# The local mask of the last attention stage: added by VectorE in PSUM instead of multiplied in by TensorE

## The reference, cut to what matters

```
DIM, DEPTH, HEADS, DIM_HEAD, WINDOW, QK_SCALE = 128, 6, 16, 64, 32, 8.0
def local_attention(q, k, v):            # q, k, v: b, h, n, d; n = 256 in windows of 32
    bq = q.reshape(b, h, nw, w, d)
    bk2, bv2 = look(bk), look(bv)        # each window sees itself and the one before: 64 keys
    mask = (it < jb) | (it > jb + w) | (jb == -1)
    sim = jnp.einsum('bhwie,bhwje->bhwij', bq, bk2) * QK_SCALE
    sim = jnp.where(mask, -jnp.finfo(sim.dtype).max, sim)
    attn = jax.nn.softmax(sim, -1)
    return jnp.einsum('bhwij,bhwje->bhwie', attn, bv2).reshape(b, h, n, d)
def attn_layer(x, ...):
    q, k, v = split(x @ Wqkv[i])         # 128 -> 3 x 1024
    q, k = l2norm(q) * qs, l2norm(k) * ksc   # then the rotary turn with its scales
    return local_attention(q, k, v) @ Wo[i]
def ffn_layer(x, ...):                   # layer norm, then a * gelu(gate)
    a, gate = split(xn @ W1[i] + b1[i])
    return a * jax.nn.gelu(gate, approximate=False) @ W2[i] + b2[i]
for i in range(DEPTH):
    x = attn_layer(shift_tokens(x), ...) + x
    x = ffn_layer(shift_tokens(x), ...) + x
```

## Time and profile before

| | |
|---|---|
| median of 3 runs | 4949.91 us (4947.79 to 4951.49) |
| the profiled execution | 4954.48 us, of which the span from the first to the last instruction is 4953.2 us |
| mean granted TensorE clock in it | 0.977 of full speed |
| last stage (`L3f`) | from about 1650 us to the end |
| busy: PE, PEld, DVE, ACT, POOL | 4669.7, 3168.2, 3438.3, 3509.7, 3707.7 us |

### The profile page before, as it was taken

The page is one execution under the profiler, slowest core; times in us unless marked ns, Lnnn a source line. Parts: engine busy times, 40 slices in busy tenths (PEclk is TensorE's granted clock), DMA queues, the critical chain, the costliest instruction groups (busy, mean ns, idle before and its releaser), DMA issues.

```text
span 4953.2 us, 115870 instructions
## 1 busy us (share of the span) xinstructions
PE 4669.7 (94%) x45088; PEld 3168.2 (64%) x45088; DVE 3438.3 (69%) x4939; ACT 3509.7 (71%) x6742; POOL 3707.7 (75%) x2336
## 2 busy tenths in 40 slices
PE   6999789996888699999999999999999999999997
PEld 4665558884444366666666666666666666666665
DVE  4553446665999677777777777777777777777774
ACT  2443655554777478778888888888877888887885
POOL 1111224445999789999999999999999999999993
PEclk9999889997999899999999999999999999999999
DMA  0000000002343222232222222232223222222222
GB/s 23 2 1 1 7 14 1 1 1 112 139 170 137 58 62 53 65 78 61 63 65 67 69 65 62 54 82 66 54 65 78 61 64 65 67 69 65 61 54 50
DMA packets 163477, 288.98 MB, mean 58 GB/s; under 512 B 44143, under 2 KB 60278, under 8 KB 158838
## 3 DMA queue, kind: packets, MB, share of 16 engines
q1 hardware_dynamic: 161926, 281.18, 21.6%
q10 hardware_dynamic: 1008, 0.39, 0.0%
HBM read 90.09 MB, written 2.62 MB: 19 GB/s over the span
## 4 chain that ended last, share of the span: by engine, by line
PE 64%; ACT 1%; POOL 1%; issue 1%; DVE 1%; DMA 0%; ACTq 0%; DVEq 0%
PE ps L2461 21%; PE ps L2519 8%; PE ps L2493 8%; PE ps L2474 7%; PE ps L2532 7%; PE ps L2506 4%; PE ps L2558 3%; PE ps L2574 3%; PE ps L2565 2%; PE ps L2488 2%; PE ps L2545 1%; PE ps L2539 1%; POOL L3f_t L3049 0%; POOL L3f_raw L3066 0%; DMA L3f_qks<-in_L_ffn_k_scale 0%
## 5 line engine op out<-in xcount | busy, mean ns | idle before, releaser
L3049 POOL TENSOR_TENSOR L3f_t<-L3f_raw,L3f_rot 128x512 f32<-128x512 f32 x768 | 1100.7, 1456 | 291.3 <-DVE L3f_raw L2876 288.8
L2461 PE MATMUL ps<-L3f_wqkv,all_z 128*128 128x512 f32 x2304 | 1171.9, 608 | 31.1 <-DVE L3f_raw L2876 22.4
L3066 POOL TENSOR_TENSOR L3f_raw<-L3f_raw,L3f_t 128x1024 f32<-128x1024 f32 x384 | 954.8, 2487 | 3.8
L3058 POOL TENSOR_TENSOR L3f_raw<-L3f_raw,L3f_rot 128x1024 f32<-128x1024 f32 x384 | 910.1, 2370 | 3.8
L2876 DVE TENSOR_TENSOR L3f_raw<-ps,L3f_ri 128x512 f32<-128x512 f32 x768 | 507.2, 682 | 273.6 <-ACT L3f_ri L2683 250.2
L2859 DVE TENSOR_REDUCE L3f_ss<-L3f_sqr 128x8 f32<-128x512 f32 x768 | 510.3, 679 | 218.3 <-ACT L3f_sqr L2673 217.1
L2704 ACT ACTIVATE L3f_qz<-ps 64x512 f32<-64x512 f32 x768 | 450.8, 587 | 179.0 <-PE ps L2474 174.4
L2474 PEld LDWEIGHTS ps<-all_ident,L3f_raw 128*128 128x128 f32 x3072 | 371.1, 141 | 293.7 <-issue 263.8
L2461 PEld LDWEIGHTS ps<-L3f_wqkv,all_z 128*128 128x128 f32 x2304 | 386.7, 191 | 263.4 <-issue 165.2
L2673 ACT ACTIVATE L3f_sqr<-ps 128x512 f32<-128x512 f32 x768 | 452.5, 596 | 67.7 <-PE ps L2461 61.3
L2725 ACT ACTIVATE L3f_pT<-ps 64x512 f32<-64x512 f32 x768 | 454.0, 591 | 55.4 <-PE ps L2506 46.4
(11 more groups left out here) (342 smaller groups left out, 8564.9 us busy)
## 6 DMA issues: line engine op xcount, KB each, us to landing
L3f_vw<-L3f_v SPq DMA_DIRECT2D x1344, 128.0 KB, 2.4
L3a_Bs<-L3a_rows SPq DMA_DIRECT2D x16, 2048.0 KB, 7.1
L3a_Cs<-L3a_rows SPq DMA_DIRECT2D x16, 2048.0 KB, 11.6
L3f_vw<-L3f_v SPq DMA_DIRECT2D x192, 64.0 KB, 2.1
L3f_wqkv<-in_L_ffn_Wqkv SPq DMA_DIRECT2D x24, 256.0 KB, 2.8
L3f_wqkv<-in_L_ffn_Wqkv SPq DMA_DIRECT2D x6, 512.0 KB, 3.6
L3f_wo<-in_L_ffn_Wo SPq DMA_DIRECT2D x48, 64.0 KB, 2.3
out<-all_x SPq DMA_DIRECT2D x8, 256.0 KB, 3.1
```

The lines of the kernel that those rows point to most:

```text
L2461: p.matmul(PS[:, j % 3, :], Z[:, u % NSEQ, t * P:t * P + P], w, start=True, stop=True).then_inc(proj.sem)
L3049: op = g.tensor_tensor(t[:, :, to], r[:, :, fr], w[:, 1, to].unsqueeze(1).broadcast_to((P, H, WIN)), ALU.mult)
L3058: g.tensor_tensor(r, r, w[:, 0, :].unsqueeze(1).broadcast_to((P, H, HD)), ALU.mult).then_inc(cosined.sem)
L3066: g.tensor_tensor(r, r, t, ALU.add).then_inc(rotated.sem)
```

## The change

The two bf16 mask products ahead of the scores are gone; the 64 score products write the banks afresh. A new VectorE step `hidden(u, t)` waits for the scores and adds `lmaskb` to banks 6 and 7 in place, broadcast over the heads; it raises a new semaphore `s_mask`, for which `top` now waits. The four lists are printed in a new order. The rest of the diff consists of such moves; TensorE's list is shown as it now stands (the step names alone, (0) for the even unit 2i, (+1) for 2i+1, and so on).

```
@@ scores, on TensorE
-                for b in range(2):
-                    p.matmul(PS[:, 6 + b, :], self.identb[:, :], lmaskb[:, t, b, :].unsqueeze(1).broadcast_to((P, PAIRS, KEYS)),
-                             start=True, stop=False, skip_group_check=True)
                 for a in range(PAIRS):
                     for w in range(NW):
                         r = slice(w % 2 * HD, w % 2 * HD + HD)
                         mm = p.matmul(PS[r, 6 + w // 2, a * KEYS:(a + 1) * KEYS], qz[:, t, a, w, :, :].rearrange("p h q -> p (h q)"),
-                                      kT[:, a, t * P + w * WIN:t * P + w * WIN + KEYS], start=False, stop=True, skip_group_check=True)
+                                      kT[:, a, t * P + w * WIN:t * P + w * WIN + KEYS], start=True, stop=True)
                 mm.then_inc(scored.sem)
@@ on VectorE
+            def hidden(u, t):
+                if not 0 <= u < N:
+                    return
+                v.wait_ge(*scored.at(u, t))
+                x = PS[:, 6:8, :].rearrange("p b (a k) -> p b a k", k=KEYS)
+                v.tensor_tensor(x, x, lmaskb[:, t, :, :].unsqueeze(2).broadcast_to((P, 2, PAIRS, KEYS)), ALU.add).then_inc(s_mask.sem)
+
             def top(u, t):
                 if not 0 <= u < N:
                     return
-                v.wait_ge(*scored.at(u, t))
+                v.wait_ge(*s_mask.at(u, t))
```

More of the change, by code:

```diff
@@ L2591, in turn_back @@
                     mm.then_inc(z_turned.sem)
-            project_out(2 * i)
+            project(2 * i + 2, "v1b")
+            ffn_up(2 * i - 1, 0)
+            ffn_up(2 * i - 1, 1)
+            ffn_up(2 * i - 1, 2)
+            centre(2 * i)
+            project(2 * i + 3, "q0a")
+            project(2 * i + 3, "q0b")
+            turn_qk(2 * i + 2, 0, 0)
+            project(2 * i + 3, "k0a")
+            variance(2 * i)
             turn_qk(2 * i + 2, 0, 1)
[L2595 to L2598, removed]
             turn_back(2 * i - 1, range(FINAL - 1))
@@ L2650, in pe @@
             ffn_gate(2 * i + 1, 1)
-            project(2 * i + 4, "v1b")
             ffn_gate(2 * i + 1, 2)
[L2653 to L2659, removed]
+            project_out(2 * i + 2)
         def act(i):
@@ L2777, in gelu @@
                     a.preload_act_table_set(EXP_LN)
[L2779 removed]
+            value(2 * i + 2, "v1a")
+            gelu(2 * i - 1, 0)
+            gelu(2 * i - 1, 1)
+            gelu(2 * i - 1, 2)
+            centred(2 * i)
+            value(2 * i + 2, "v1b")
+            squared(2 * i + 3, "q0a")
+            squared(2 * i + 3, "q0b")
             turned(2 * i + 2, 0, 0)
@@ L2956, in dve @@
                 rotation(2 * i // NSEQ + 1)
-            sums(2 * i + 3, "k0a")
+            total(2 * i + 1, 1)
             share(2 * i + 1, 0)
+            share(2 * i + 1, 1)
+            norm(2 * i + 2, "k1a")
+            norm(2 * i + 2, "k1b")
+            scale(2 * i + 1, 0)
+            residual(2 * i)
+            gated(2 * i - 1, 0)
+            gated(2 * i - 1, 1)
+            gated(2 * i - 1, 2)
+            sums(2 * i + 3, "q0a")
+            sums(2 * i + 3, "q0b")
+            bounded(2 * i + 3, "q0")
+            scale(2 * i + 1, 1)
             norm(2 * i + 3, "q0a")
-            residual(2 * i)
             norm(2 * i + 3, "q0b")
[L2962 to L2967, removed]
+            normal(2 * i)
             land(2 * i - 1, range(FINAL - 1))
@@ L2970, in dve @@
             land(2 * i - 1, range(FINAL - 1, FINAL))
-            normal(2 * i)
-            share(2 * i + 1, 1)
-            scale(2 * i + 1, 1)
+            sums(2 * i + 3, "k0a")
+            sums(2 * i + 3, "k0b")
+            bounded(2 * i + 3, "k0")
+            norm(2 * i + 3, "k0a")
+            norm(2 * i + 3, "k0b")
+            hidden(2 * i + 2, 0)
+            top(2 * i + 2, 0)
             sums(2 * i + 3, "q1a")
             sums(2 * i + 3, "q1b")
-            top(2 * i + 2, 0)
             bounded(2 * i + 3, "q1")
+            norm(2 * i + 3, "q1a")
+            norm(2 * i + 3, "q1b")
             below(2 * i + 2, 0)
-            norm(2 * i + 3, "q1a")
             sums(2 * i + 3, "k1a")
-            norm(2 * i + 3, "q1b")
             sums(2 * i + 3, "k1b")
@@ L2992, in dve @@
             norm(2 * i + 4, "q0a")
+            sums(2 * i + 4, "k0a")
+            share(2 * i + 2, 0)
+            residual(2 * i + 1)
+            norm(2 * i + 4, "q0b")
+            sums(2 * i + 4, "k0b")
             total(2 * i + 2, 1)
-            share(2 * i + 2, 0)
-            norm(2 * i + 4, "q0b")
-            residual(2 * i + 1)
             scale(2 * i + 2, 0)
-            sums(2 * i + 4, "k0a")
-            sums(2 * i + 4, "k0b")
             bounded(2 * i + 4, "k0")
```

130 lines of the change are left out of this document (60 added, 70 removed).

## The result

The changed kernel takes 4898.6 us (median of 4 runs, 4895.76 to 4900.73) beside 4950.7 us for the kernel before: a ratio of 0.9887 with a 95% interval of [0.9863, 0.9911]. That is 52 us less by the medians and 56 by the ratio. The forecast was 4879 us. The time lies in the range, 20 us above the forecast and just above what rival A allowed (4862 to 4895), at the lower edge of rival B's price.

What follows compares the result with a forecast made beforehand. TensorE's packed order in the last stage was taken to bound the kernel. From 4954.5 us profiled, less 80 for the mask products, plus 9 for waits, gives 4883, about 4879 us as median; range 4855 to 4940 us.

Steps and rivals of the forecast that it cites:

- rival A: Last stage: TensorE stays packed, with small waits only; 4862 to 4895 us, chance 0.68.
- rival B: New lists too tight: late norms, turns and `spread` take 0.85 us an iteration; 4910 us (4895 to 4940), chance 0.16.
- What bounds the kernel: Last stage: TensorE's order is packed, iteration 67.08 us; the stage costs the sum of its streams.
- rival D: No change: GpSimd's chain sets the period, iteration stays about 67 us; 4950 us, chance 0.06.
- The cost of a mask pair, 0.43 us: In `scores`, two 512-column bf16 products cost 0.43 us a call, 187 packed calls: 80 us.
- the low end of the range: No waits, long `scale` gone, `values` and `scores` side by side sharing a change of tile: 4855 us.
- `hidden` at 1.22 us, off TensorE's path: VectorE's mask add takes 1.22 us a call, 5.04 us an iteration with starts, beside TensorE's work.
- the charge for the orders: New lists: a few places even within 0.3 us cost 0.2 us an iteration, 9 us.
- its sign: Profile after: TensorE waits naming ScalarE's turned or spread outputs would point to rival B.
- The place that it watched most closely: Behind `project_out(2i+1)`, before `scores(2i+3, 1)`: VectorE needs 12.7 us, TensorE 12.8, even within 0.3 us.
- What the profile after would show: No L2488, TensorE 800 of 800 us, iteration 65.4 to 65.7 us, VectorE near 54.5, `hidden` 1.22.
- Fill and drain: Outside the packed stretch: new worth as much as old within 3 us; long `scale` 7 us both ways.

Runs made afterwards that it cites:

- f3: f1's lists, but masking by the two bf16 products on TensorE and no VectorE add: 4928.3 us, ratio 0.9955.
- f1: Changed kernel with all four lists laid out anew by its own profile's durations, every step kept: 4823.4 us, ratio 0.9745.
- e2: Changed kernel with its new lists, without the VectorE add, so no mask at all: 4896.0 us, ratio 0.9885.
- e3: Kernel before with its old lists, the VectorE add straight ahead of each row maximum replacing the mask products: 4909.9 us, ratio 0.9912.
- e1: Kernel before with its old lists, the two mask products taken out and no mask in their place: 4879.9 us, ratio 0.9853.
- x2: Changed kernel with the add done twice in each call: 4935.8 us, ratio 0.9972.
- e4: Changed kernel's new lists, masking by the two bf16 products on TensorE as before, no add: 4991.2 us, ratio 1.0076.
- x1: Changed kernel without the first of four ScalarE copies of `spread` in the even unit's first half: 4868.0 us, ratio 0.9837.
- f2: Changed kernel with all four lists laid out anew, a second layout with somewhat more distance between steps: 4876.5 us, ratio 0.9853.

## Why the prediction was right, and where its sizes were wrong

- **What bounds the kernel** was right. With the products gone and no waits the iteration falls by all that they cost (f3 to f1), with GpSimd at 761 of 800 us; rival D is out.
- **The cost of a mask pair, 0.43 us,** was right for the calls that stand alone. Where `values` comes directly before, it is 0.69. The prediction had seen that these two could share a change of tile, and put it only into the low end of the range. The removal was worth 1.99 us an iteration, not 1.72. The Trainium skill's 131 ns for a product ("TensorE: Matmul & The Clock Gate", Back-to-back issue gap) in a real stream would have made it an estimated 1.05; the 0.43 us for two products here, 0.215 each, do not bear it out.
- **`hidden` at 1.22 us, off TensorE's path,** was right (1.224 us; e2 against the changed kernel: no difference). That holds for the new lists; in the old ones the add costs 30 us (e3 against e1). x2 shows that of 5.04 us more an iteration 4.1 would be hidden too.
- **The step that failed is the charge for the orders: "I charge 0.2 us an iteration for them, 9 us."** It measured 0.86 us an iteration and 38 us (e4 against before). That this is half of 1.72, what rival B took, is chance; but the mechanism is B's, turns that wait for ScalarE behind `spread` and `turned`, and the prediction had named those outputs as its sign. So what came true is in the main the rival that it gave 0.16, and the range held because it took B in; A, given 0.68, was missed by 4 us. The place that it watched most closely, VectorE behind `project_out(2i+1)`, did not wait: from `residual` to the end of `below` VectorE took 12.2 us (3169.74 to 3181.94), not 12.7, and `scores(2i+3, 1)` started 1.2 us later, 0.70 of which was the wait for ScalarE. Without that wait (x1) it does not wait either. It had laid VectorE's and GpSimd's lists beside TensorE's in numbers, and not ScalarE's.
- That the forecast is only 20 us off is partly luck, since the two errors partly cancel: forecast 67.08 - 1.72 + 0.2 = 65.56, measured 67.07 - 1.99 + 0.86 = 65.94. The profiled execution was to be 71 us shorter and was 53.8. The 17 us are 45 x 0.38 = 17, 3 for the iterations with `rotation` and 2.6 for counting 46.7 packed iterations where 45 are, less the 5.6 that fill and drain gave. The rest of the 20 is that the median lies 2 us below the profiled execution, not 4.6.
- **What the profile after would show:** `hidden` at 1.22, no L2488, 0.09 us ahead of `scores` (3040.62 to 3041.15, for a `turn_qk` of 0.44) and VectorE near 54.5 us (54.3; 56.5 in the stretch with `rotation`) came true. TensorE at 800 of 800 and 65.4 to 65.7 us did not.
- **Fill and drain** were to be equal within 3 us, with 7 more for the long `scale`: up to the first `ffn_out` 3.4 us were gained, although the long `scale` stayed (9.80 us), and behind the 45 iterations 2.2.

That `spread` makes the 0.70 us wait is shown by x1. That `turned` makes the one of 0.29 us is read from the rows, and it is gone in f1, but no run changes it alone.

## What to carry to other kernels

Where one engine is packed, a new hand-written order must be followed on every engine that gives its buffers back, the one with the most idle time too: a row of copies, 2.4 us long, is a wall for whoever stands behind it, whatever the busy share. Take the two parts of a change apart (new order with the old work, old order with the new work) before judging either: here the new order by itself cost 38 us, and the add was free only in it; in the old order it cost 30. f1 shows that an order can hide the add without that price. Where a bank of a packed engine comes back late, look at distances between starts: the wait view gave TensorE's waits 0.53 us an iteration, the starts 0.99.

## What the hardware showed that was not expected

**Copies of 64 partitions do not overlap on ScalarE.** In the rows above, activations over 128x512 (a copy, then a square) take 0.60 us and start 0.49 us apart (3047.50, 3047.99). Four of 64x512 take 2.40 us, and the next starts 2.43 us after the first: 0.60 each for half the data. `spread` and `turned` (`qz`) are 32 such copies in an iteration. The cause is not shown. One candidate: each of these copies writes the other half of the partitions than the one before. For VectorE, the Trainium skill has a rule of this kind ("VectorE: DVE Perf Modes", Two Vector instructions with no wait between them): an instruction that starts on another quadrant than the one before is held until that one has finished. No run here tests it on ScalarE.

**A VectorE instruction with two SBUF operands waits for GpSimd, and may miss its turn.** The kernel before had one `scale` of 8.44 us, and the prediction saw no other like it. The changed kernel has one of 9.80 us in its fill; VectorE, then GpSimd, then TensorE in their order of time:

```profile
1713.22 9.80 DVE L2916 TENSOR_TENSOR L3f_sm<-L3f_sm,L3f_sl 128x1024 f32<-128x1024 f32 x1
```

```profile
1712.53 2.37 POOL L3066 TENSOR_TENSOR L3f_raw<-L3f_raw,L3f_rot 128x1024 f32<-128x1024 f32 x1
1714.87 2.47 POOL L3057 TENSOR_TENSOR L3f_t<-L3f_raw,L3f_rot 128x512 f32<-128x512 f32 x2
1717.31 2.33 POOL L3074 TENSOR_TENSOR L3f_raw<-L3f_raw,L3f_t 128x1024 f32<-128x1024 f32 x1
1719.61 2.33 POOL L3066 TENSOR_TENSOR L3f_raw<-L3f_raw,L3f_rot 128x1024 f32<-128x1024 f32 x1
```

```profile
1723.08 1.97 PE L2503 MATMUL ps<-all_ident,L3f_sm 128*128 128x128 f32 x8 [7.19 <-DVE L3f_sm L2916]
```

GpSimd runs five instructions back to back until 1721.94, then idles; `scale` ends 1.08 us after that. Alone it takes 1.22 us. In the middle of the stage it happens on a smaller scale, here in the changed kernel, VectorE first and then GpSimd:

```profile
3005.73 3.02 DVE L2916 TENSOR_TENSOR L3f_sm<-L3f_sm,L3f_sl 128x1024 f32<-128x1024 f32 x1
```

```profile
3005.31 2.35 POOL L3074 TENSOR_TENSOR L3f_raw<-L3f_raw,L3f_t 128x1024 f32<-128x1024 f32 x1
```

GpSimd ends at 3007.66, `scale` at 3008.75. This is no accident: in the changed kernel 54 of the 192 `scale` take over 1.6 us, in f2 181, and every one of them ends 1.08 to 1.09 us after a GpSimd instruction has ended. So f2's longer `scale` is that its order puts nearly all of them beside a GpSimd instruction.

The Trainium skill ("SBUF — State Buffer", SBUF: two separate sides) calls it an exclusive lock: a VectorE instruction with two SBUF inputs and a GpSimd one that reads SBUF share a pair of ports, and the later one is blocked until the first has ended. The 3.02 us agree; the 9.80 us go past the rule, since the waiting `scale` let four more GpSimd instructions go first. All of e1, e2, e3, e4 and x2 have one such long `scale` in the fill (7.5 to 9.1 us), x1, f1, f2 and f3 have none; what decides it was not found.
